# Cross attention in a two-layer decoder: the first eight heads' values and denominators from one product, with slots, sends and bias moved on GpSimd

## Chip, cores, metric

The kernel runs on one NeuronCore of a Trainium2 chip. The metric is the device time of one execution in microseconds (us). Engines are called TensorE (PE, with its weight loads PEld), VectorE (DVE), ScalarE (ACT), GpSimd (POOL) and SyncE (SP). Each has its own instruction stream, runs it in order, and waits for semaphores that others count up.

## The reference

The input x is 8 batches of 256 tokens of width 256, in float32; a context of 77 rows per batch goes with it. The decoder has two layers, each with a self attention, a cross attention to the context and a mixture of experts (8 experts, the best 2 for each token), each with a layer norm in front and a residual. The change lies in the cross attentions, 16 heads of 16 columns:

```python
q = (query @ wq.T + bq)...; k = (key @ wk.T + bk)...; v = (value @ wv.T + bv)...
scores = einsum('bhqd,bhkd->bhqk', q, k) / sqrt(HD)
attn = softmax(scores)
ctx = einsum('bhqk,bhkd->bhqd', attn, v)
return ctx @ wo.T + bo
```

## The kernel before

`attention_crossed` runs once per layer (names L0x and L1x, 237 to 362 us and 1094 to 1232 us of the trace with what surrounds it). A unit u is half a batch: b = u // 2 is the batch and c = u % 2 the half of the heads, eight in each. Five engine programs go through u = 0 to 15 side by side.

TensorE's order in a unit is: scores of unit u+1 (L827), transposes of the maxima (L837), the products of the list `mid`, then the turned scores of u, laid out with the 77 keys on the partitions (L850), and the values. The values of a first half (c = 0) come behind the turned scores of the second half; the values of a second half come ahead of the turned scores of the next batch's first half. Everything goes through a ring of seven PSUM banks, and the values have one bank more, `ps_o`. A values group (L865) is eight products with `v_s`, whose weights hold two heads for 32 rows of output, and eight with `half_ones`, which sum the exponentials into the denominators, the same rows 256 columns further on. Each product gives two records.

The other products are: `q`, `v` and `x` for the batches ahead (L300, L288, L293), `k` for a group of batches (L282), the projection `o` of batch b-1 in the second half (L797), and three steps of the router: `r0` transposes the normalized rows (L804), `r1` gives the logits (L809), `r2` counts how many tokens went to each expert (L815).

VectorE in unit u takes the maximum of scores u+1 (L468), adds the shift of u into `q_m` (L475), copies keys, takes statistics, and then: in a first half `slots(b-3)`, and behind it the orders and snapshots of the experts (`ORDER_BY = 2`, so at b = 5; `FULL_BY = [3, 4]`, at b = 6 and 7); in a second half `choose(b-2)` (best two experts), `add(b-1)` (residual L498, statistics L501, L506). Last in each unit are the sums of unit u-1: a reciprocal of the denominators (L480) and the product into `o_t` (L483). `slots` makes from gates (L536 to L538) and counts (L541 to L546) each token's row in the expert table. After the last unit come `slots(5)`, the first expert rows, `last_sums` (L490, L491), the hidden rows of the first early expert block, `choose(6)` and `add(7)`.

ScalarE takes products out of PSUM, normalizes (L205, L627) and exponentiates four banks per unit (L667). GpSimd does the small steps of the norms (L255 to L258), the bias on the residual (L725), and sends the routed rows to the table by four indirect DMAs per batch (L744). In a first half it has `spread_norm(b+2)` and `send(b-3)`; in a second half `bias(b)` and `route_norm(b-1)`.

SP's program in the stage is this loop. It stores each batch (L446), loads the first two experts' weights (L1912 to L1916) when the order is known, and for b = 4 and b = 5 waits until the batches up to 3 and 4 are scattered, then loads early expert rows (L2167):

```python
for b in range(B):
    eng.wait_ge(added, b + 1)
    eng.dma_start(... X[:, tiles, :]).then_inc(route["kept"], 16)
    if b == ORDER_BY + 1:
        experts["first_loads"](eng)
    for i, last in enumerate(FULL_BY):
        if b == last + 1:
            for par in range(2):
                eng.wait_ge(scattered[par], ((last - par) // 2 + 1) * 64)
            experts["load_early"](eng, i)
```

Behind the last unit TensorE starts on the early expert blocks while batches 6 and 7 are still being routed.

## Time and profile before

| what | us |
|---|---|
| three runs | 1500.22, 1502.38, 1503.75 (median 1502.38) |
| the profiled execution, its own time | 1504.03 |
| its span, first to last instruction | 1502.4 |
| mean granted TensorE clock | 0.993 |
| busy: PE / VectorE / ScalarE / GpSimd | 1433.9 / 748.7 / 619.1 / 490.5 |
| first cross stage, 228 to 362 | PE 122.0, VectorE 110.2, ScalarE 79.9, GpSimd 51.2 of 134 |
| second cross stage, 1078 to 1216 | PE 125.9, VectorE 109.3, ScalarE 78.1, GpSimd 51.3 of 138 |

Times in the trace count from the start of the span. A timeline row gives start, duration, engine, line, operation, output and inputs with their shapes, how many instructions it merges, and in brackets how long the engine had been idle before it and what released it. Records of TensorE overlap, because its products are pipelined. "remote" is a releaser that the profile can't name.

### The profile page before, as it was taken

What the parts mean: (1) busy time and instruction counts of PE and PEld (TensorE: products, weight loads), DVE (VectorE), ACT (ScalarE), POOL (GpSimd) and SP (SyncE); (2) the same over time, 40 slices, a digit from 0 to 9 for tenths busy, and PEclk for the clock granted to TensorE, in tenths of its full rate; (3) what the DMA queues carried; (4) which work ended last, traced back from release to release, by engine and by line L of the source; (5) the groups of instructions that cost most, each with busy time, mean ns of one, the idle gap of its engine ahead of it and who ended that gap; (6) DMA issues with size and microseconds to landing.
All of it is one profiled execution on the core that took longest, in us unless ns stands there. A gap on an engine that the chain in (4) does not pass through costs nothing. (4 is left out here: it accounts for less than half of the span.)

```text
span 1502.4 us, 34667 instructions
## 1 busy us (share of the span) xinstructions
PE 1433.9 (95%) x11880; PEld 1159.7 (77%) x11881; DVE 748.7 (50%) x2160; ACT 619.1 (41%) x1711; POOL 490.5 (33%) x758
## 2 busy tenths in 40 slices
PE   7999998988999999999999999999899899999998
PEld 5676766767899999976777777777666579999997
DVE  6666757887433333344444444444278862222222
ACT  2433346653222222235445444545366533333332
POOL 3545442444322122223233233333224452222222
PEclk9999999999999999999999999999999999999999
DMA  9920000152243434120000000000001522533332
GB/s 316 333 69 2 2 2 9 45 176 62 50 119 67 144 71 114 32 64 1 0 1 1 1 1 1 1 1 0 1 16 44 174 78 40 149 93 94 94 90 34
DMA packets 79666, 97.46 MB, mean 65 GB/s; under 512 B 10523, under 2 KB 72579, under 8 KB 79555
## 3 DMA queue, kind: packets, MB, share of 16 engines
q1 hardware_dynamic: 64643, 77.58, 16.4%
q0 software_dynamic: 13680, 17.19, 6.6%
q8 instruction: 73, 1.20, 0.3%
q10 hardware_dynamic: 1232, 1.18, 0.2%
q14 instruction: 38, 0.31, 0.1%
HBM read 57.51 MB, written 39.59 MB: 65 GB/s over the span
## 5 line engine op out<-in xcount | busy, mean ns | idle before, releaser
L1741 POOL TENSOR_TENSOR L1a_prob<-L1a_prob,L1a_rtot 128x1024 f32<-128x1024 f32 x64 | 121.1, 1892 | 275.8 <-DVE L1a_rtot L1614 275.8
L2270 PEld LDWEIGHTS L0x_ps<-L0f_rows_t,L0f_w_up 128*128 128x128 f32 x1584 | 183.7, 193 | 10.4 <-issue 9.0
L2270 PE MATMUL L0x_ps<-L0f_rows_t,L0f_w_up 128*128 128x128 f32 x1584 | 185.8, 277 | 5.6 <-issue 4.8
L2346 ACT ACTIVATE L1f_hid<-L1x_ps,L1f_b_up 128x128 f32<-128x128 f32 x296 | 92.4, 363 | 163.0 <-PE L1x_ps L2270 159.7
L2270 PEld LDWEIGHTS L1x_ps<-L1f_rows_t,L1f_w_up 128*128 128x128 f32 x1184 | 139.5, 194 | 3.4 <-issue 1.6
L2270 PE MATMUL L1x_ps<-L1f_rows_t,L1f_w_up 128*128 128x128 f32 x1184 | 140.4, 277 | 0.6 <-ACT L1f_rows_t L2330 0.6
L2279 PE MATMUL L1x_ps<-L1f_w_down,L1f_hid 128*128 128x256 f32 x592 | 134.1, 380 | 1.9 <-issue 1.9
L2214 POOL TENSOR_TENSOR turn<-eps 128x1 f32<-128x1 f32 x74 | 13.6, 184 | 372.3 <-DVE wv L2448 367.7
L1683 ACT ACTIVATE L1a_prob<-L1a_ps_s,L1a_nmax 128x256 f32<-128x256 f32 x256 | 118.2, 473 | 38.1 <-DVE L1a_nmax L1609 38.1
L2279 PEld LDWEIGHTS L1x_ps<-L1f_w_down,L1f_hid 128*128 128x128 f32 x592 | 109.6, 190 | 15.5 <-issue 2.1
L1245 POOL TENSOR_SCALAR_AFFINE_SELECT L0a_prob<-L0a_prob 128x128 f32<-128x128 f32 (+1 forms) x256 | 79.8, 353 | 104.3 <-ACT L0a_prob L1199 104.3
L2338 ACT ACTIVATE ctx_in<-L0x_ps 128x256 f32<-128x256 f32 x72 | 27.6, 383 | 183.1 <-PE L0x_ps L2270 157.1
L2279 PE MATMUL L0x_ps<-L0f_w_down,L0f_hid 128*128 128x256 f32 x432 | 99.4, 380 | 1.7 <-DVE L0f_hid L2435 1.7
L1199 ACT ACTIVATE L0a_prob<-L0a_ps 128x384 f32<-128x384 f32 x128 | 52.4, 497 | 108.0 <-PE L0a_ps L1331 108.0
L1609 DVE TENSOR_REDUCE L1a_nmax<-L1a_ps_s 128x2 f32<-128x512 f32 x128 | 79.2, 681 | 31.4 <-PE L1a_ps_s L1805 31.4
L2279 PEld LDWEIGHTS L0x_ps<-L0f_w_down,L0f_hid 128*128 128x128 f32 x432 | 79.3, 190 | 11.2 <-DVE L0f_hid L2435 1.9
L1819 PEld LDWEIGHTS L1a_ps_t<-ident,L1a_prob 128*128 128x128 f32 x500 | 59.6, 141 | 34.6 <-issue 26.3
L2435 DVE TENSOR_TENSOR L0f_hid<-ctx_in,L0x_ps 128x256 f32<-128x256 f32 x72 | 30.2, 420 | 106.0 <-ACT ctx_in L2338 70.1
L1819 PE MATMUL L1a_ps_t<-ident,L1a_prob 128*128 128x128 f32 x500 | 76.9, 276 | 3.3 <-DVE L1a_prob_t L1618 2.4
L1618 DVE COPY L1a_prob_t<-L1a_ps_t 128x512 f32<-128x512 f32 x63 | 42.8, 680 | 58.3 <-PE L1a_ps_t L1819 58.3
L1693 ACT ACTIVATE L1a_prob_t<-L1a_ps_t 128x512 f32<-128x512 f32 x62 | 37.1, 598 | 81.5 <-PE L1a_ps_t L1819 81.5
L2425 DVE TENSOR_SCALAR token<-L1f_from_end 128x1 int32<-128x1 f32 x37 | 5.7, 153 | 126.8 <-DMA out_dram<-wv,token 126.8
(486 smaller groups left out, 2812.5 us busy)
## 6 DMA issues: line engine op xcount, KB each, us to landing
expert_table<-zero SPq DMA_DIRECT2D x1, 16640.0 KB, 68.5
L0f_w_up<-in_w_dram SPq DMA_DIRECT2D x8, 1408.0 KB, 6.8
L1f_w_up<-in_w_dram SPq DMA_DIRECT2D x8, 1024.0 KB
L1f_w_down<-in_w_dram SPq DMA_DIRECT2D x8, 1024.0 KB
L0f_w_down<-in_w_dram SPq DMA_DIRECT2D x8, 768.0 KB, 8.7
L1f_rows<-expert_table SPq DMA_DIRECT2D x35, 130.0 KB
L0f_rows<-expert_table SPq DMA_DIRECT2D x32, 130.0 KB
sums<-X SPq DMA_DIRECT2D x8, 256.0 KB
```

The costliest lines, as they stand in the source:

```text
L1199: eng.activation(prob[u % 2][:, r, :, :], bank("p", u, r)[:, 0:KT * W].rearrange("p (t w) -> p t w", t=KT), ACT.Exp).then_inc(exp_done, 1)
L1245: ins = eng.affine_select(out=p, in_=p, compare_op=ALU.is_ge, fill=0.0, base=base, pattern=[[0, 2], [sign, n]], channel_multiplier=-sign)
L1609: eng.tensor_reduce(nmax[:, j % RING, :], src, AX.X, ALU.max, negate=True).then_inc(max_done, 1)
L1618: eng.tensor_copy(prob_t[s % 2][:, k, :], turn_bank(b, s, k)).then_inc(even_out, 1)
L1683: ins = eng.activation(prob[:, j % RING, q, :], ps_s[:, k, q * S:(q + 1) * S], ACT.Exp, bias=nmax[:, j % RING, q:q + 1], accum_out=total[: ...
L1693: eng.activation(prob_t[s % 2][:, k, :], turn_bank(b, s, k), ACT.Copy).then_inc(odd_out, 1)
L1741: eng.tensor_tensor(v, v, r.unsqueeze(2).to_broadcast([P, 2 * QT_N, S]), ALU.mult).then_inc(norm_done, 1)
L1819: ins = eng.transpose(out[:, o:o + P], prob[:, j % RING, q, c * P:(c + 1) * P], ident[:, :])
L2270: ins = eng.matmul(ps_h[c][:, o:o + P], w_up[par][:, t, w0:w0 + P], rows_t[:, t, :], start=(t == 0), stop=(t == DT - 1))
L2279: ins = eng.matmul(ps_y[:, 0:D], hid[:, c, k * P:(k + 1) * P], w_down[par][:, 2 * c + k, :], start=(c == 0 and k == 0), stop=(c == CHUNKS ...
L2346: ins = eng.activation(hid[:, c, k * P:(k + 1) * P], ps_h[c][:, k * P:(k + 1) * P], ACT.Gelu, bias=b_up[par][:, 2 * c + k:2 * c + k + 1])
L2435: ins = eng.tensor_tensor(hid[:, c, :], mid[:, c, :], ps_h[c][:, 2 * P:4 * P], ALU.mult)
```

## The change

For the first eight heads `v_s` now holds values and ones in turn, and one group of eight products gives values and denominators together: half of the rows of each product are values, half are sums, and the other half-product has them the other way round. ScalarE copies both (`gather`) into SBUF, SP moves the sums and the values with two DMAs each to the rows where they belong (`move`), VectorE takes the reciprocal (`sums_first`), and GpSimd multiplies (`first_outputs`). The rows of `wo` and the bias of v are reordered on the host to match (`in_turn`). The second eight heads keep the old form with interleaved rows. VectorE keeps the gates, GpSimd gets the rest of `slots` for batches 0 to 4, first in its unit; `send` is split in two, tile 0 in the first half and tile 1 in the second behind `route_norm`, and the bias comes last. VectorE's sums of a second half stand ahead of the expert order and the snapshots. SP no longer loads the first weights; ScalarE issues them in units 11 and 12.

```diff
-            eng.wait_ge(v_cleared, b % 2 + 1)
+            eng.wait_ge(v_cleared, 2 * (b % 2 + 1))
             if values_free is not None:
                 eng.wait_ge(*values_free)
-            ins = eng.activation(even_odd(v_s[b % 2][0:SC, :, :]), bank[0:SC, 0:D].rearrange("p (a two d) -> p a two d", two=2, d=DH), ACT.Copy)
...
-        eng.memset(v_s[i][:, :, :], 0.0).then_inc(v_cleared, 1)
+
+        eng.memset(v_s[i][:, 0:HEADS // 2, :], 1.0).then_inc(v_cleared, 1)
+        eng.memset(v_s[i][:, HEADS // 2:HEADS, :], 0.0).then_inc(v_cleared, 1)
...
+                def move(b):
+
+                    eng.wait_ge(copied, b + 1)
+                    if b:
+                        eng.wait_ge(rsum_done, b)
+                    for w in range(HALVES):
+                        eng.dma_start(summed_t[1 - w::2, :], gathered[w::2, w, :]).then_inc(sums_moved, 16)
+                    if b:
+                        eng.wait_ge(first_out, b)
+                    for w in range(HALVES):
+                        eng.dma_start(valued_t[1 - w::2, :], gathered[1 - w::2, w, :]).then_inc(values_moved, 16)
+
+                move(0)
                 for b in range(B):
+                    if b + 1 < B:
+                        move(b + 1)
                     eng.wait_ge(added, b + 1)
                     tiles = slice(b * QT_N, (b + 1) * QT_N)
                     eng.dma_start(route["sums"].rearrange("(t p) d -> p t d", p=P)[:, tiles, :], X[:, tiles, :]).then_inc(route["kept"], 16)
-                    if b == ORDER_BY + 1:
-                        experts["first_loads"](eng)
                     for i, last in enumerate(FULL_BY):
                         if b == last + 1:
                             for par in range(2):
...
+                def sums_first(b):
+                    eng.wait_ge(sums_moved, 32 * (b + 1))
+                    if b:
+                        eng.wait_ge(first_out, b)
+                    eng.reciprocal(rsum_first[:, :], summed_t[:, :]).then_inc(rsum_done, 1)
+
                 def sums(u):
                     b, c = part(u)
                     eng.wait_ge(values_done, u + 1)
                     linked(eng.reciprocal(rsum[:, :], ps_o[:, S:2 * S]))
-                    if c == 0 and b:
+                    if b:
                         eng.wait_ge(projected, b)
...
+                        eng.wait_ge(slot_done, b)
...
+                def gates(b):
...
+                    gate = xr[:, b % 2, :, GATE:GATE + TOP]
                     linked(eng.tensor_scalar(first_gate[:, :], odds[:, :], 1.0, None, ALU.add))
                     linked(eng.reciprocal(gate[:, :, 0], first_gate[:, :]))
-                    eng.tensor_tensor(gate[:, :, 1], gate[:, :, 0], odds[:, :], ALU.mult)
+                    eng.tensor_tensor(gate[:, :, 1], gate[:, :, 0], odds[:, :], ALU.mult).then_inc(gates_done, 1)
...
+                    gates(b)
+                    eng.wait_ge(slot_done, b)
...
+                        if b:
+                            sums_first(b - 1)
                         if b + 2 < B:
                             first["statistics"](eng, b + 2)
                         if b >= 3:
-                            slots(b - 3)
+                            gates(b - 3)
+                        if b:
+                            sums(u - 1)
+                        if b >= 3:
...
-                        if u == units - 1:
-                            sums(u - 1)
                         if b >= 1:
                             add(b - 1)
-                    if u and u < units - 1:
-                        sums(u - 1)
                 slots(B - 3)
+                sums_first(B - 1)
                 x["take_early"](0)
                 last_sums()
...
+                def gather(b):
+
+                    eng.wait_ge(values_done, CHUNKS * b + 1)
+                    if b:
+                        eng.wait_ge(sums_moved, 32 * b)
+                        eng.wait_ge(values_moved, 32 * b)
+                    eng.activation(gathered, ps_o[:, :].rearrange("p (w s) -> p w s", w=HALVES), ACT.Copy).then_inc(copied, 1)
+
...
+                    if c == 1:
+                        gather(b)
                     if u == units - 1:
                         x["table"]()
                     for t in of(END, u):
                         take(t)
+                    for e in range(2):
+                        if u == 2 * (ORDER_BY + 3) + 1 + e:
+                            experts["first_load"](eng, e)
                     if c == 0 and b + 2 < B:
...
+                def first_outputs(b):
+
+                    eng.wait_ge(values_moved, 32 * (b + 1))
+                    eng.wait_ge(rsum_done, b + 1)
+                    if b:
+                        eng.wait_ge(projected, b)
+                    eng.tensor_tensor(o_t[:, 0, :], valued_t, rsum_first, ALU.mult).then_inc(first_out, 1)
...
+                    taken = route["taken"]
+                    eng.wait_ge(both_done, b + 1)
+                    wait_out(eng, "r2", b)
+                    for q in range(QT_N):
+                        eng.tensor_tensor(place[:, q, :], counts[:, 0, q, :], taken[:, :], ALU.add)
+                        linked(eng.tensor_tensor(taken[:, :], counts[:, 1, q, :], taken[:, :], ALU.add))
+                    linked(eng.tensor_tensor(picked[:, :, :, :], chosen[:, :, :, :],
+                                             place[:, :, :].unsqueeze(1).to_broadcast([P, TOP, QT_N, EXPERTS]), ALU.mult))
+                    for n in (4, 2):
+                        linked(eng.tensor_tensor(picked[:, :, :, 0:n], picked[:, :, :, 0:n], picked[:, :, :, n:2 * n], ALU.add))
+                    linked(eng.tensor_tensor(slot_f[:, :, :], picked[:, :, :, 0], picked[:, :, :, 1], ALU.add))
+                    eng.tensor_copy(slot_i[:, b % 2, :, :], slot_f[:, :, :].rearrange("p k t -> p t k")).then_inc(slot_done, 1)
...
+                    eng.wait_ge(gates_done, b + 1)
...
+                        if b >= 3:
+                            slots(b - 3)
+                        if b:
+                            first_outputs(b - 1)
                         if b + 2 < B:
                             first["spread_norm"](eng, b + 2)
                         if b >= 3:
-                            send(b - 3)
+                            send(b - 3, [0])
                     else:
-                        bias(b)
                         if b >= 1:
                             route_norm(b - 1)
+                        if b >= 3:
+                            send(b - 3, [1])
+                        bias(b)
                 x = experts["pool_parts"](eng)
+                first_outputs(B - 1)
...
-                        eng.wait_ge(o_out, CHUNKS * (t[1] + 1) - last)
+                        eng.wait_ge(first_out, t[1] + 1)
+                        if not last:
+                            eng.wait_ge(o_out, t[1] + 1)
...
+                    flat = v_s[b % 2][0:SC, :, :].rearrange("p h n -> p (h n)")
+                    if c == 1:
+                        eng.wait_ge(copied, b + 1)
+                    elif b:
+                        eng.wait_ge(o_out, b)
+                    for summed in range(c + 1):
                         for w in range(HALVES):
                             for r in range(GROUPS):
-                                lhs = half_ones[0:SC, w, :] if summed else v_s[b % 2][0:SC, c * 8 + 2 * r + 1 - w, :]
-                                ins = eng.matmul(ps_o[rows(r), summed * S:(summed + 1) * S], lhs, prob[u % 2][0:SC, r, w * S:(w + 1) * S],
-                                                 start=(w == 0 and not summed), stop=(w == HALVES - 1), skip_group_check=True)
+                                o = (summed if c else w) * S
+                                n = 2 * DH * (c * 8 + 2 * r + 1 - w) - (1 - w)
+                                lhs = half_ones[0:SC, w, :] if summed else flat[:, n:n + 2 * DH]
+                                ins = eng.matmul(ps_o[rows(r), o:o + S], lhs, prob[u % 2][0:SC, r, w * S:(w + 1) * S],
+                                                 start=(c == 0 or w == 0 and not summed), stop=(c == 0 or w == HALVES - 1), skip_group_check=True)
                     ins.then_inc(values_done, 1)
 
...
-    def first_loads(eng):
+    def first_load(eng, e):
 
         eng.wait_ge(listed["ordered"], 1)
-        for e in range(2):
-            load_weights(eng, e, e)
+        load_weights(eng, e, e)
 
...
-                eng.memset(half_ones[:, w, 16 * (1 - w):16 * (2 - w)], 1.0).then_inc(halves, 1)
+                eng.memset(half_ones[:, w, 1 - w::2], 1.0).then_inc(halves, 1)
...
-        env.update(y=wv0[:, 0, :])
+        env.update(y=wv0[:, 0, :], rsum_first=wv0[:, 1, :], gathered=wk0[:, :, :], summed=wo0[:, 0, :], valued=wo0[:, 1, :])
...
+    def in_turn(w):
+
+        return w.reshape(-1, 2, 16, *w.shape[1:]).swapaxes(1, 2).reshape(w.shape)
```

## Rows read from the trace of the kernel before

**Rows 1.** The page, part 1: busy us, share of the span, instructions.
```profile
PE 1433.9 (95%) x11880; PEld 1159.7 (77%) x11881; DVE 748.7 (50%) x2160; ACT 619.1 (41%) x1711; POOL 490.5 (33%) x758
```
**Rows 2.** Busy time by stretch: PE, PEld, DVE, ACT, POOL, clock, DMA share, GB/s.
```profile
252.00:267.00 15.00, 14.75 (x180) 10.46 (x176) 12.01 (x31) 10.02 (x21) 3.85 (x9) 1.00 0.06 20
...
1208.00:1214.00 6.00, 4.95 (x38) 2.95 (x39) 5.07 (x21) 1.68 (x5) 2.44 (x5) 0.57 0.25 83
```
**Rows 3.** Timeline, batches 6 and 7 of the first layer.
```profile
334.32 1.10 PE L850 MATMUL L0x_ps<-L0x_q_m,L0x_k_m 32*77 32x256 f32 x16 [1.78 <-DVE L0x_q_m L475]
...
339.49 1.43 DVE L468 TENSOR_REDUCE L0x_tops<-L0x_ps 128x16 f32<-128x1232 f32 x1
...
340.84 0.68 DVE L475 TENSOR_TENSOR L0x_q_m<-L0x_q_m,L0x_ps 128x512 f32<-128x512 f32 x1
...
348.07 1.10 PE L850 MATMUL L0x_ps<-L0x_q_m,L0x_k_m 32*77 32x256 f32 x16
...
353.46 1.07 PE L865 MATMUL L0x_ps_o<-L0x_prob,L0x_v_s 77*32 77x256 f32 x16 [1.61 <-DVE L0x_o_t L483]
```
**Rows 4.** Timeline, batches 4 and 5: the expert order and what waited.
```profile
309.45 0.16 DVE L1963 TENSOR_TENSOR L0r_tokens<-taken,regions 128x8 f32<-128x8 f32 x1
...
312.53 0.15 DVE L1976 TENSOR_SCALAR L0r_least<-L0r_least 128x1 f32<-128x1 f32 x1
...
315.08 1.97 PE L797 MATMUL L0x_ps<-wo,L0x_o_t 128*128 128x256 f32 x8 [2.12 <-DVE L0x_o_t L483]
...
317.41 1.10 PE L850 MATMUL L0x_ps<-L0x_q_m,L0x_k_m 32*77 32x256 f32 x16
...
318.53 2.04 ACT L667 ACTIVATE L0x_prob<-L0x_ps 77x512 f32<-77x512 f32 x4 [0.41 <-PE L0x_ps L850]
```
**Rows 5.** The bank of the values by instruction: ns min/median/max, first and last start.
```profile
L865 PE MATMUL L0x_ps_o<-L0x_prob,half_ones x256: 378/379/380, 238.7 to 355.0; 77*32 77x256 f32 x128
...
L480 DVE RECIPROCAL L0x_rsum<-L0x_ps_o x15: 1722/1756/1758, 239.8 to 351.1; 128x256 f32<-128x256 f32 x15
L483 DVE TENSOR_TENSOR L0x_o_t<-L0x_ps_o,L0x_rsum x15: 423/424/425, 241.6 to 352.9; 128x256 f32<-128x256 f32 x15
```
**Rows 6.** GpSimd's lines, ns min/median/max; an early load, KB and us to landing.
```profile
L725 POOL TENSOR_TENSOR X<-X,bo x16: 1265/1272/1290, 234.2 to 1203.8; 128x512 f32<-128x512 f32 x16
...
L255 POOL TENSOR_TENSOR L0x_r_veps<-L0x_r_mv,eps x8: 194/194/195, 253.1 to 367.1; 128x2 f32<-128x2 f32 x8
...
L744 POOL DMA_INDIRECT expert_table<-L0x_xr,L0x_slot_i x32: 959/966/1244, 277.1 to 382.9; - x32
...
ctx_in<-expert_table SPq DMA_DIRECT2D x8, 130.0 KB, 2.1
```
**Rows 7.** Timeline, the router's norm of batch 5.
```profile
337.16 0.25 DVE L506 BATCH_NORM_AGGREGATE L0x_r_mv<-L0x_r_stats 128x2 f32<-128x6 f32 x2
...
338.84 0.22 POOL L258 TENSOR_SCALAR L0x_r_shift_by<-L0x_r_offset 128x2 f32<-128x2 f32 x1
```
**Rows 8.** Timeline, the last send of batch 3 and SP's next issue.
```profile
330.42 0.96 POOL L744 DMA_INDIRECT expert_table<-L0x_xr,L0x_slot_i  x1 [0.30 <-issue]
...
333.70 0.89 SPq L2167 DMA_DIRECT2D ctx_in<-expert_table  x2
```
**Rows 9.** The copy of the experts' numbers, ns min/median/max.
```profile
L522 DVE CAST L0x_index_f<-L0x_index x8: 169/170/1782, 265.8 to 374.6; 128x4 f32<-128x4 uint32 x8
```
**Rows 10.** SP's issues of the first experts' weights, both layers.
```profile
313.34 0.38 SPq L1913 DMA_DIRECT2D L0f_w_down<-in_w_dram  x1
...
315.48 0.02 SPq L1912 DMA_DIRECT2D L0f_w_up<-in_w_dram  x1
...
1174.97 4.22 SPq L1915 DMA_DIRECT2D L1f_b_up<-in_b_dram  x1
```
**Rows 11.** Timeline behind the last unit: last sums, batch 7's router rows.
```profile
356.49 0.95 DVE L490 RECIPROCAL L0x_rsum<-L0x_ps_o 128x128 f32<-128x128 f32 x1
...
369.99 0.63 PE L804 MATMUL L0x_ps<-ident,L0x_xr 128*128 128x128 f32 x4 [0.20 <-ACT L0x_xr L627]
```

More of the change, by code:

```diff
@@ L138, in batches_of @@
         return b0, b1, b1 - b0
-    def even_odd(v):
-        return v.rearrange("p (a two) (half d) -> p a (two half) d", two=2, half=2)[:, :, 0::3, :]
     def weights_in(eng):
@@ L374, in attention_crossed @@
         apart, odds, first_gate = sb("apart", [P, QT_N]), sb("odds", [P, QT_N]), sb("first_gate", [P, QT_N])
+        gathered, summed_t, valued_t, rsum_first = (env[k] for k in ("gathered", "summed", "valued", "rsum_first"))
         cleared = sem("cleared")
+        gates_done, link_p = sem("gates_done"), sem("link_p")
+        copied, sums_moved, values_moved = sem("copied"), sem("sums_moved"), sem("values_moved")
+        rsum_done, first_out = sem("rsum_done"), sem("first_out")
         scores_done, max_done = sem("scores"), sem("max")
@@ L529, in choose @@
                     eng.tensor_copy(xr[:, par, :, TOKEN], route["from_end"][:, b * QT_N:(b + 1) * QT_N])
+                def gates(b):
+                    eng.wait_ge(odds_done, b + 1)
+                    gate = xr[:, b % 2, :, GATE:GATE + TOP]
+                    linked(eng.tensor_scalar(first_gate[:, :], odds[:, :], 1.0, None, ALU.add))
+                    linked(eng.reciprocal(gate[:, :, 0], first_gate[:, :]))
+                    eng.tensor_tensor(gate[:, :, 1], gate[:, :, 0], odds[:, :], ALU.mult).then_inc(gates_done, 1)
                 def slots(b):
                     par, taken = b % 2, route["taken"]
-                    eng.wait_ge(odds_done, b + 1)
-                    gate = xr[:, par, :, GATE:GATE + TOP]
-                    linked(eng.tensor_scalar(first_gate[:, :], odds[:, :], 1.0, None, ALU.add))
-                    linked(eng.reciprocal(gate[:, :, 0], first_gate[:, :]))
-                    eng.tensor_tensor(gate[:, :, 1], gate[:, :, 0], odds[:, :], ALU.mult)
+                    gates(b)
+                    eng.wait_ge(slot_done, b)
                     wait_out(eng, "r2", b)
@@ L566, in _ @@
                         if b >= 3:
-                            slots(b - 3)
+                            gates(b - 3)
+                        if b:
+                            sums(u - 1)
+                        if b >= 3:
+                            if b == 3 and not final or b - 3 == ORDER_BY or b - 3 in FULL_BY:
+                                eng.wait_ge(slot_done, b - 2)
                             if b == 3 and not final:
@@ L633, in odds_of @@
                     if b:
-                        eng.wait_ge(slot_done, b)
+                        eng.wait_ge(gates_done, b)
                     eng.wait_ge(apart_done, b + 1)
@@ L858, in values @@
                     wait_out(eng, "v", b)
-                    if u:
-                        eng.wait_ge(o_out, u)
-                    for summed in range(2):
+                    flat = v_s[b % 2][0:SC, :, :].rearrange("p h n -> p (h n)")
[4 more added lines that the diff above has]
+                    for summed in range(c + 1):
                         for w in range(HALVES):
                             for r in range(GROUPS):
-                                lhs = half_ones[0:SC, w, :] if summed else v_s[b % 2][0:SC, c * 8 + 2 * r + 1 - w, :]
-                                ins = eng.matmul(ps_o[rows(r), summed * S:(summed + 1) * S], lhs, prob[u % 2][0:SC, r, w * S:(w + 1) * S],
-                                                 start=(w == 0 and not summed), stop=(w == HALVES - 1), skip_group_check=True)
+                                o = (summed if c else w) * S
[3 more added lines that the diff above has]
+                                                 start=(c == 0 or w == 0 and not summed), stop=(c == 0 or w == HALVES - 1), skip_group_check=True)
                     ins.then_inc(values_done, 1)
```

17 lines of the change are left out of this document (12 added, 5 removed).

## The prediction, made before the changed kernel ran

> **What bounds the kernel now.** The page comes first: TensorE (PE) is busy for 1434 of 1502 us [rows 1], so the program is nearly PE-bound. Then the view of busy time by stretch: in the first cross attention, 252 to 267 us, PE is busy 14.75 of 15 us, while GpSimd has 3.85 and VectorE 12.0 [rows 2]. There a PE instruction removed is time won. The other end of the stage is different. The timeline shows PE waiting: 2.12 us for the scaled outputs of VectorE before L797, 1.78 us for the shift before L850, and 1.61 us for `o_t` before the last values [rows 3, 4]. So from batch 5 on what counts is who comes late, and I read both crosses (237 to 362 us and 1094 to 1232 us) batch by batch. I call R the start of the turned scores of a batch's second unit (317.41, 334.32 and 348.07 for batches 5, 6, 7) [rows 3, 4].
>
> **Products removed.** For the first eight heads the second group of products with `half_ones` goes: 16 records of 379 ns each, overlapping four at a time [rows 5]. The group at 353.46 spans 1.07 us [rows 3], with the tail of its last product, which the next one runs under; four at a time make 16 x 379 / 8 = 0.76 us at least. I take 0.93 us per batch (bounds 0.76 and 1.07), nearer to the span. The group stands just after R.
> Batches 0 to 2: PE is the bound, VectorE, ScalarE and GpSimd have room. The new path must be in time: ScalarE's copy 128x512 comes behind the exponentials, which end at R+3.2 (318.53+2.04) [rows 4]; the copy has no row of its own here, bounds are 0.42 (the 256-column read of the same bank on VectorE [rows 5]) and 1.27 (512 columns on GpSimd [rows 6]); I take 0.6, since the exponential of 512 columns takes 0.51 (2.04/4). SP issues two DMAs, they land after 2.1 us (130 KB [rows 6]; 64 KB may do it in less, 3 us under load is the upper bound), at R+6.3. The reciprocal on VectorE from SBUF: 1.75 us from PSUM [rows 5], I take the same; bounds 0.9 and 1.8. It ends at R+8.1; the statistics and sums of the other half end at R+11.5; L797 wants them at about R+11.7. Just in time: **3 x 0.93 = -2.8 us** per layer (0 if landing takes 3 us).
>
> **Work moved to GpSimd.** Slots: nine dependent instructions; an instruction of two columns takes 0.195 us there, 512 columns 1.27 [rows 6], so 0.2 to 0.26 each, with gaps 2.3 us. The outputs' product of 256 columns: between, (1.27+0.195)/2 = 0.73. Per batch GpSimd then has 2.3+0.73, two norms of 1.6 (337.41 to 339.06 [rows 7]), sends 4x1.27 = 5.1 (0.97 and a gap of 0.30 [rows 6, 8]), bias 1.27: 12.5 us in a period of 14.8. That fits, with about 2 us spare; the bias last frees the router's norm. The bias collision on VectorE (a cast of 1782 ns instead of 169 [rows 9]) goes away, but stood beside PE's work: 0.
> Batch 3: the router's rows hang on the keys' products, which are not moved; PE waited for them already, so the 0.93 only lengthens that wait: 0.
> Batch 4 into 5: the expert order on VectorE, 309.45 to 312.68 = 3.2 us [rows 4], stood before the sums and made PE wait 2.12. Now it stands behind them, but ahead of the next maximum (1.43) and shift (0.68) [rows 3]: they end at R+17.2 against 18.0 before: **-0.8**, in the second layer **-0.9**.
>
> **Expert weights issued by ScalarE.** In unit 11 the load stands ahead of the router's norm. On SP 1.8 us passed from the end of the first expert's issues (313.72) to the second's first (315.48), most of it the load of the expert's number, and two issues take about 0.8; in the second layer there are four issues, and one of them stood for 4.22 us with the queue full [rows 10]. So ScalarE gets to the norm 2 to 4 us late, and PE's L804 with it. Against that stands batch 5's 0.93 and the 1.78 us wait before L850. I take **-0.8** in the first layer and **+1.1** in the second.
>
> **What is queued behind SP's waits.** This decides. SP's program runs: move(b+1), wait for added(b), store, and for b=4 and 5 a wait for the scatters of batches up to 3 and 4, then the early expert rows. Before, nothing urgent stood behind that wait. Now move(6) and move(7) do. And what it waits for became later: tile 1 of batch 3 is sent only in unit 13, behind the router's norm. Numbers for batch 6 (R=334.32): the aggregate ends at R+3.1 (337.16+0.25) [rows 7], norm 1.6, two sends to R+7.1. From the end of the last send to SP's next issue it was 2.3 us (331.38 to 333.70), and the two loads took 0.9 [rows 8]: SP is free at R+10.4, issues, and the sums land at R+12.8. VectorE gets there at about R+5.2: the shift ended at 341.52 = R+7.2, behind a sum of 2.17 us that is gone [rows 3, 5] (0.2 allowed for what comes in between). It waits **7.5 us** in the one queue that also holds gates, the other sums, snapshot and the last shift. From 12.8: reciprocal 1.75, gates 0.6, sum 2.2, so `o_t` at R+17.4; L797 can't start before; snapshot 0.9 and shift 0.7 end at 19.1. Before, the batch took 348.07-334.32 = 13.75 [rows 3]; now 19.2: **+5.5 us** per layer. Nothing covers it: L797 and the turned scores behind it are all that PE has left in the unit.
> Batch 7 repeats it: send(4) tile 1 leaves at R+7.0, SP is free at 10.2, sums land at R+12.7. They stand ahead of `last_sums`, which began at 356.49 = R+8.4 [rows 11] and now begin at R+14.5; the expert products' hidden rows stand behind them. PE has up-products, r0 and r1 until about R+12; the last router rows were turned at 369.99 = R+21.9 [rows 11]; behind GpSimd's send(5) (from R+15.2 to 20.3), odds and norm they come at R+24.7: **+2.8 us**. The 1.61 us that the last values waited [rows 3] are won, but only in front of that wait.
> Clock: after such a hole PE fell to the lower level (1.2 GHz): mean 0.57 in 1208 to 1214 [rows 2], where the last values stood. That costs 0 to 3.4 us a layer more than before; I take **+1.0**.
>
> **Sum.** First layer -2.8-0.8-0.8+5.5+2.8+1.0 = +4.9; second -2.8-0.9+1.1+5.5+2.8+1.0 = +6.7; together +11.6. The profiled execution took 1504.0 (span 1502.4), so 1515.6; the three runs' median is 1502.4, 1.6 lower: **1514**.
>
> A rule against the change: the Trainium skill, DMA: Bandwidth & Descriptors (Anatomy of one DMA), says that a semaphore wait happens on the issuing sequencer before dispatch, not in the DMA engines. By this rule everything behind SP's wait stands still; were it not so, the +5.5 and +2.8 would be 0.
>
> **Rivals.**
> (A) *The blocked queue costs little* and the savings show. For it: PE is the bound in most of the stage. Against: VectorE is in order, and the sums are asked for before all else in the unit. It would take the sends landing by R+6. Then batches 0 to 2, 4 and 5 keep their gain and the last values come 1.6 us sooner: -6.0 and -4.2, so **1492**. Chance 0.17.
> (B) *VectorE's reciprocal now holds GpSimd up*, on top of the forecast. Its source and its result are in SBUF now. A cast of VectorE stood 1.6 us too long beside GpSimd's bias [rows 9], so the engines can block each other. If GpSimd's bias waits 1.15 us in batches 3 to 6, its 2 us of room go, and the xn and slot path adds about 0.9 a batch: 4x0.9x2 = +7, **1521**. Chance 0.13.
> The Trainium skill, SBUF — State Buffer (SBUF: two separate sides), has such a rule: a pair of ports that VectorE and GpSimd share is locked for a whole instruction. The trace agrees for the cast, 1782 against 169 ns; for a long reciprocal no row shows it.
> (C) *It evens out*: the block is half as long, because the last scatter lands sooner than the 2.3 us [rows 8] and GpSimd sends it earlier. Half of 2x8.3 is 8.3 less, and with it the clock's 2.0: 1514-10.3 = 1503.7, **1504**. Chance 0.10.
>
> **Chances.** Forecast 0.60. A measurement of this kernel can tell about 0.2%, 3.0 us, from no change. Slower: forecast and B, 0.73; same: C, 0.10; faster: A, 0.17. The range goes from 1499 (landing 2.1 us, shorter block, no clock loss) to 1525 (B and two clock drops); it leaves out A.
>
> **What would show it.** Right: VectorE idle 6 to 8 us before the new reciprocal in the units after batches 6 and 7, released by a DMA from `wk0`'s columns, in both layers; SP's issues of these moves directly behind the early expert rows; PE's hole in front of L797 of batch 6; batch periods shorter by 0.9 us for batches 0 to 2. Wrong: those moves issued within 1 us of their copies (then A), or GpSimd idle nowhere and VectorE waiting for its product (then B), or unit 11's norm on time.

## The result, and the profile after

Three runs of the changed kernel took 1581.32, 1582.49 and 1587.34 us, against 1500.22, 1502.38 and 1503.75 before: a ratio of 1.054 (95% interval 1.051 to 1.058), 80 us slower. The forecast was 1514 with a range to 1525. The sign was right, but 68 us of the 80 were not in it; as e1 and e9 below show, the sign too owed most to effects that the forecast had small or at nothing. The profiled execution is the one of 1582.49 us, with a span of 1580.8.

The page of the changed kernel, part 1 (busy us, share of the span, instructions):

```profile
span 1580.8 us, 34355 instructions
PE 1468.0 (93%) x11624; PEld 1178.9 (75%) x11625; DVE 734.2 (46%) x2074; ACT 625.8 (40%) x1727; POOL 520.6 (33%) x868
```

TensorE has 256 records fewer than in [rows 1], 128 products at two records each, and is busy 34 us longer. Next, busy time by stretch, from the start of the first cross stage to the first down-product of the experts (columns as in [rows 2]). The kernel before:

```profile
228.00:365.20 137.20, 125.18 (x1412) 89.40 (x1411) 111.79 (x320) 80.60 (x171) 52.71 (x87) 0.99 0.22 76
```

The changed kernel, with 10 us from the middle of it:

```profile
228.00:401.80 173.80, 137.54 (x1282) 94.57 (x1281) 103.74 (x278) 83.80 (x179) 67.49 (x140) 0.83 0.22 72
340.00:350.00 10.00, 5.78 (x48) 2.98 (x52) 3.17 (x5) 3.81 (x7) 3.17 (x6) 0.50 0.45 159
```

The same work takes 36.6 us more. 24.2 of them are idle time of TensorE (36.3 against 12.0), and 12.4 are products that run longer although there are fewer: the mean granted clock is 0.83. The last row, the 10 us around the end of an idle stretch of 9.2 us (it ends at 344.22), has a granted clock of 0.50 throughout, the lower level (1.2 GHz). The second layer loses 42 us.

I compare batch by batch, by the time from the turned scores R of a batch's second unit to those of the next. The rows are starts of L850 (L938 after), subtracted:

```
                  batch 0->1   1->2   2->3   3->4   4->5   5->6   6->7
before, layer 1      14.80  14.95  16.01  16.81  18.03  16.91  13.75
after,  layer 1      15.48  14.08  15.15  27.20  21.32  26.65  22.29
before, layer 2      14.80  14.94  16.02  16.97  16.76  16.92  13.74
after,  layer 2      14.76  14.21  15.15  27.91  24.12  29.85  21.98
```

Up to batch 3 the kernel is a little faster, by 1.0 and 1.6 us per layer where the forecast had 2.8. From the first batch in which sends run beside routing, each period is 3 to 13 us longer. What TensorE waits for there is named by the view of waits, first layer, changed kernel (us in total, times, longest):

```profile
PE L0x_ps L892 <- ACT L0x_xr L662: 24.1, 5, 9.2
PE L0x_ps_o L897 <- DVE L0x_o_t L517: 5.1, 1, 5.1
```

L892 turns the normalized router rows (`r0`), L662 is ScalarE's normalization. The view of L662 says what ScalarE waited for:

```profile
L662 ACT ACTIVATE L0x_xr<-X,L0x_r_shift_by,L0x_r_rstd x16: 584/599/617, 255.1 to 405.5; 128x256 f32<-128x256 f32 x16
...
  DMA expert_table<-L0x_xr,L0x_slot_i: 28.2, 5
  DMA expert_table<-L1x_xr,L1x_slot_i: 25.6, 5
```

and the timeline of batch 5, first layer, shows how:

```profile
332.06 0.25 DVE L532 BATCH_NORM_AGGREGATE L0x_r_mv<-L0x_r_stats 128x2 f32<-128x6 f32 x2
332.92 0.42 ACTq L2005 DMA_DIRECT2D L0f_w_up<-in_w_dram  x1
332.95 1.10 SPq L456 DMA_DIRECT2D wo<-wk  x2
333.75 0.23 POOL L256 TENSOR_SCALAR L0x_r_shift_by<-L0x_r_offset 128x2 f32<-128x2 f32 x1
334.78 1.06 POOL L823 DMA_INDIRECT expert_table<-L0x_xr,L0x_slot_i  x1 [0.81 <-issue]
336.15 0.96 POOL L823 DMA_INDIRECT expert_table<-L0x_xr,L0x_slot_i  x1 [0.30 <-issue]
337.13 1.27 POOL L773 TENSOR_TENSOR X<-X,bo 128x512 f32<-128x512 f32 x1
340.34 1.75 DVE L501 RECIPROCAL wv<-wo 128x256 f32<-128x256 f32 x1 [5.47 <-DMA wo<-wk]
342.98 1.09 ACT L662 ACTIVATE L0x_xr<-X,L0x_r_shift_by,L0x_r_rstd 128x256 f32<-128x256 f32 x2 [9.88 <-DMA expert_table<-L0x_xr,L0x_slot_i]
344.22 1.08 PE L892 MATMUL L0x_ps<-ident,L0x_xr 128*128 128x128 f32 x4 [9.20 <-ACT L0x_xr L662]
345.23 1.94 PE L958 MATMUL L0x_ps_o<-L0x_prob,L0x_v_s 77*32 77x256 f32 x16
```

The router's rows live in two buffers, `xr[b % 2]`. ScalarE may write the rows of batch b only when those of batch b-2 have been scattered (`wait_ge(scattered[par], b // 2 * 64)` in its `route_norm`). Before, all four sends of batch b-3 left in the first half of a unit pair, and by the time of the norm of batch b-1 they had long landed. Now GpSimd issues tile 1 behind its own `route_norm(b-1)`, so ScalarE, whose next instruction is the normalization of that very batch, waits for the issue (from the shift at 333.98 to 337.11) and the landing (to 342.9). The landing is slow in this batch, 5.8 us, with the first expert's weights under way (the DMA engines are 0.92 busy from 335 to 344.2); in batch 6, without them, it took 1.7 us and ScalarE still waited 4.53. All that TensorE has behind L892 waits with it, and then runs at half clock: a values group takes 1.94 us instead of 1.07.

### The profile page after: what moved, and what is told of

It reads as the page before. It is cut to its first block and busy times, and to the rows that moved or that the text cites. A ratio compares the mean times of both kernels' runs of the same rounds, so it can differ in the third digit from the quotient of the medians.

```text
span 1580.8 us, 34355 instructions
## 1 busy us (share of the span) xinstructions
PE 1468.0 (93%) x11624; PEld 1178.9 (75%) x11625; DVE 734.2 (46%) x2074; ACT 625.8 (40%) x1727; POOL 520.6 (33%) x868
## 5 line engine op out<-in xcount | busy, mean ns | idle before, releaser
L2371 PEld LDWEIGHTS L0x_ps<-L0f_w_down,L0f_hid 128*128 128x128 f32 x432 | 79.6, 191 | 10.9 <-DVE L0f_hid L2527 1.7
L1201 DVE TENSOR_REDUCE L0a_tops<-L0a_ps 128x2 f32<-128x384 f32 x128 | 62.5, 552 | 11.6 <-PE L0a_ps L1407 11.6
```

What stands on the lines that cost most here:

```text
L1201: eng.tensor_reduce(tops[u % UNITS][:, :, at_row], src, AX.X, ALU.max, negate=True).then_inc(max_done, 1)
L2371: ins = eng.matmul(ps_y[:, 0:D], hid[:, c, k * P:(k + 1) * P], w_down[par][:, 2 * c + k, :], start=(c == 0 and k == 0), stop=(c == CHUNKS ...
```

## The experiments

I call W the theory that this wait makes the loss, and S the one of the forecast, SP's blocked queue. All edits are to the changed kernel unless it is said. The kernel before ran again beside each group of experiments: its medians are 1499.5 (e1 to e4), 1501.3 (e6 to e8), 1503.6 (e9, e10) and 1499.6 (e11, e12). A difference between kernels of different groups carries this drift of up to 4 us, so I also give the distance to the kernel before of the same group. That distance was 80.1 us for the changed kernel. "Batch 5's period" is the column 5->6 of the table above. e2, e3 and e4 are single executions.

**e1: sends together.**

```diff
-                            send(b - 3, [0])
+                            send(b - 3)
...
-                        if b >= 3:
-                            send(b - 3, [1])
```

> Edit: the changed kernel with all four sends of batch b-3 in the first half again; nothing else. Theory W: what costs the 78 us is ScalarE's normalization of a batch's router rows, which waits until the rows of two batches before have been scattered out of the same buffer; these scatters now leave in the same unit behind the router's norm on GpSimd. Then that wait goes: 1490 to 1505 us, and PE waits under 2 us per layer for the normalized rows instead of 24.1 and 22.3. Theory S: the moves behind SP's wait for the scatters hold VectorE up and that carries the loss. Here the scatter of batch 3 lands before the move of batch 6 too, so S also expects about 1500. This run alone does not tell W from S. A third theory (C): the loss is the moved slots and products on GpSimd or the contention of its port with VectorE; then it stays above 1560.

Measured: 1507.84 (ratio 1.0056, 1.0038 to 1.0073), 8.4 us above the kernel before. 72 us of the 80 are gone with this one edit. It lies inside the forecast's range, but not for the forecast's reasons, as the next runs show.

**e2: three buffers in the first layer.** `xr`, `slot_i` and `scattered` have three entries, used by `b % 3`, in the first layer; the second keeps two.

```diff
-        xr, xr_t = sb("xr", [P, 2, QT_N, ROW]), sb("xr_t", [P, DT, S])
+        xr, xr_t = sb("xr", [P, 2 if final else 3, QT_N, ROW]), sb("xr_t", [P, DT, S])
```

> Edit: the changed kernel with three buffers for the router's rows and slots in the first layer only; the sends stay apart, so SP's waits and the place of each send are as changed. The second layer keeps two buffers, as a control. W: ScalarE's wait for a scatter goes in the first layer and stays in the second: 28 to 36 us off the 1582, so 1546 to 1554; the second layer's batches keep their 22 to 30 us periods. What then stays in the first layer is S's part: VectorE's wait of 5 to 8 us for the moved sums of batches 6 and 7. S (SP's blocked queue carries most): at most 5 us off, 1577 or more.

Measured: 1560.34. It is 22 us less, not 28 to 36; the first layer's seven periods are 21.4 us shorter. The view of ScalarE's normalization has no wait for a scatter left in the first layer, and the control is untouched:

```profile
  DMA expert_table<-L1x_xr,L1x_slot_i: 24.5, 5
  POOL L0x_r_shift_by L256: 5.2, 4
```

What stays in the first layer is largely S, now in the open. VectorE's reciprocal of the moved sums, batches 5, 6 and 7:

```profile
328.70 1.75 DVE L501 RECIPROCAL wv<-wo 128x256 f32<-128x256 f32 x1 [5.54 <-DMA wo<-wk]
350.32 1.75 DVE L501 RECIPROCAL wv<-wo 128x256 f32<-128x256 f32 x1 [7.88 <-DMA wo<-wk]
371.94 1.75 DVE L501 RECIPROCAL wv<-wo 128x256 f32<-128x256 f32 x1 [4.35 <-DMA wo<-wk]
```

In batches 6 and 7 SP issued the moves 7.26 and 6.20 us behind ScalarE's copy, which is S. In batch 5 it issued them 0.03 us behind it, so the 5.54 us are not S (e6 shows what they are). The forecast had 7.5 us for batch 6. The period from batch 6 to 7 is 21.96 us against 13.75 before, 8.2 more where the forecast took 5.5, and the first down-product starts at 380.6 instead of 365.2, 15 us late.

**e3: the kernel before with its sends parted.**

```diff
-                            send(b - 3)
+                            send(b - 3, [0])
                     else:
                         bias(b)
                         if b >= 1:
                             route_norm(b - 1)
+                        if b >= 3:
+                            send(b - 3, [1])
```

> Edit: the kernel before, with only the sends parted: tile 1 of batch b-3 in the second half, behind the router's norm. There are no moves on SP here. W: the whole loss without the rest of the change: 60 to 80 us above the kernel before, 1560 to 1582, with PE waiting 20 to 25 us per layer for the normalized rows. S: nothing urgent stands behind SP's wait, so within 4 us of 1502.

Measured: 1571.21, 72 us above the kernel before, with nothing else of the change in it. The periods from batch 3 on are 26.83, 17.57, 26.60 and 21.53. The normalization, line by its two layers:

```profile
  DMA expert_table<-L0x_xr,L0x_slot_i: 29.0, 5
  DMA expert_table<-L1x_xr,L1x_slot_i: 28.9, 5
```

72 from this edit and 8 from all the rest (e1) make the 80. W is shown by taking the wait away in two ways (e1 by the place of the sends, e2 by a third buffer) and by adding it alone.

**e4: early rows one batch later.** SP's wait for the scatters and the loads behind it stand behind the next `move`.

```diff
-                        if b == last + 1:
+                        if b == last + 2:
```

> Edit: the changed kernel, with SP's wait for the scatters and the early loads one batch later, behind the next move; sends stay apart. W: ScalarE's wait is untouched, so little is won: 1572 to 1582; PE still waits 20 us or more per layer for the normalized rows, and only VectorE's 5 to 8 us waits for the moved sums go. S: 1500 to 1515.

Measured: 1569.16, 13 us less (10 by the distances): more than W allowed, far from S. The normalization still waits 26.0 us in the first layer. VectorE's waits for the sums of batches 6 and 7 are gone (0.68 and none instead of 8.36 and 5.47), but that of batch 5 is 7.00, so it had another cause. The first layer's periods are no shorter for it (142.1 us in sum, 142.2 in the changed kernel), since ScalarE's wait covers them; what is won lies mostly behind the last turned scores, where the first down-product comes 15.2 us after the R of batch 7 instead of 23.5, and 15.2 instead of 20.3 in the second layer.

**e6: the first weights behind the move.** e1, and SP issues both experts' weights behind the store of batch 4.

```diff
+                    if b == ORDER_BY + 2:
+                        for e in range(2):
+                            experts["first_load"](eng, e)
...
-                        if u == 2 * (ORDER_BY + 3) + 1 + e:
-                            experts["first_load"](eng, e)
```

The rows that led to it, e1's timeline: ScalarE's weights and SP's moves of batch 5 leave in the same microsecond, and the sums land 6.6 us after their second issue.

```profile
319.03 0.42 ACTq L2003 DMA_DIRECT2D L0f_w_up<-in_w_dram  x1
319.06 1.10 SPq L456 DMA_DIRECT2D wo<-wk  x2
...
326.21 1.75 DVE L501 RECIPROCAL wv<-wo 128x256 f32<-128x256 f32 x1 [5.23 <-DMA wo<-wk]
```

> Edit: sends together as in e1, and the first two experts' weights no longer issued by ScalarE in units 11 and 12 but by SP behind the store of batch 4, so behind the move of batch 5 in its queue. Theory M: in e1 the moves of batch 5 (64 KB each) were issued at the same moment as the first expert's weights (2.2 MB) and landed 6.6 us later instead of 1.9, which made VectorE wait 5.2 and 5.9 us, and in the second layer ScalarE's issues of four loads took 5.1 us and held the normalization up by 5.2. Then both go: batch 5's period falls from 19.07 and 24.99 to 16.5 to 17.5 us, together 8 to 11 us off e1's 1507.8: 1496 to 1500. Rival N: the waits come from VectorE's or GpSimd's own load (slots, blocked port); then e6 stays at 1505 to 1509.

Measured: 1506.08 (1.0023, 1.0011 to 1.0035). Batch 5 gains more than M said, 14.60 and 14.61 us instead of 19.07 and 24.99. But batch 6 now takes 19.79 and 21.01, so only 1.8 us are won (3.6 by the distances) and the number is missed. The burst has moved on to the next victim, as the second layer shows: in 10 us with the DMA engines busy throughout (a DMA share of 1.03) a scatter needs 7.4 us to land, and SP is held in one issue for 6 us.

```profile
1185.00:1195.00 10.00, 6.02 (x66) 4.00 (x64) 6.91 (x22) 3.87 (x10) 6.24 (x17) 0.96 1.03 347
```

```profile
1184.67 6.01 SPq L2006 DMA_DIRECT2D L1f_b_up<-in_b_dram  x1
...
1194.23 1.09 ACT L665 ACTIVATE L1x_xr<-X,L1x_r_shift_by,L1x_r_rstd 128x256 f32<-128x256 f32 x2 [3.36 <-DMA expert_table<-L1x_xr,L1x_slot_i]
...
1199.60 1.75 DVE L504 RECIPROCAL wv<-wo 128x256 f32<-128x256 f32 x1 [7.07 <-DMA wo<-wk]
```

**e7: e6 and e4 together.**

> Edit: e6, and SP's wait for the scatters with the early rows' loads one batch later, behind the next move. If SP's block still costs something where the sends are together (e1: VectorE waited 2.9 us for the sums of batch 6, PE 3.1 us in front of the output product), this takes 2 to 5 us more off e6: 1492 to 1497. If the early rows then come too late for the early blocks, the stage's end gives it back: equal to e6 or up to 3 us above it.

Measured: 1504.68 (1.0020, 1.0007 to 1.0033), not told apart from e6. That does not show that SP's wait costs nothing. In e6 it held the moves of batch 6 for 3.6 and 5.2 us behind ScalarE's copy. In e7 they leave at once in the first layer, but beside the weights the sums need 6.0 us to land, and VectorE waits 4.67 instead of 5.71:

```profile
333.87 0.60 ACT L707 ACTIVATE wk<-L0x_ps_o 128x512 f32<-128x512 f32 x1
334.50 1.11 SPq L456 DMA_DIRECT2D wo<-wk  x2
340.99 1.75 DVE L504 RECIPROCAL wv<-wo 128x256 f32<-128x256 f32 x1 [4.67 <-DMA wo<-wk]
```

**e9: the weights apart.** e6, with one expert behind the store of batch 4 and the other behind that of batch 5.

```diff
-                    if b == ORDER_BY + 2:
-                        for e in range(2):
+                    for e in range(2):
+                        if b == ORDER_BY + 2 + e:
```

> Edit: as e6, but SP issues the first expert's weights behind the store of batch 4 and the second's behind the store of batch 5, each behind a move. In e6 both came in one burst, the DMA engines were full for 10 us, a scatter took 7.4 us to land instead of 2.6 and batch 6 needed 19.8 and 21.0 us. Theory M (the weights' transfers are what delays moves and scatters): half the burst at a time fits between the moves, batches 5 and 6 together take 32 to 33 us instead of 34.4 and 35.6, so 3 to 6 us off e6: 1499 to 1503. Rival: the early rows' load and the wait before it in the same queue hold batch 6 up as before: 1504 to 1508, and the second expert's weights, one batch later, may hold the experts' first products up.

Measured: 1502.65 (0.9994, 0.9974 to 1.0014), even with the kernel before. Batches 5 and 6 together take 32.87 and 32.29 us. M holds: the place of 4 MB of weights is worth 5 us against e1 (9 by the distances). What is left in batch 6 is in part S: SP issues the moves 2.4 us behind the copy (2.9 in the second layer), right behind the early rows, and VectorE waits 4.19 (3.53).

```profile
332.73 0.60 ACT L707 ACTIVATE wk<-L0x_ps_o 128x512 f32<-128x512 f32 x1
335.72 1.11 SPq L456 DMA_DIRECT2D wo<-wk  x2
339.37 1.75 DVE L504 RECIPROCAL wv<-wo 128x256 f32<-128x256 f32 x1 [4.19 <-DMA wo<-wk]
```

**e8: slots on VectorE again.** e6, with `slots(b - 3)` in VectorE's first halves instead of `gates`, and gone from GpSimd.

> Edit: e6 with the slots of batches 0 to 4 on VectorE again, behind the gates. Theory: VectorE is not the bound in batches 0 to 3 and 2.3 us of slots there cost nothing; in batches 5 to 7 its queue carries the order and snapshots, so 1 to 2 us each: e6 plus 0 to 4 us. Rival B (the shared port: VectorE's reciprocal from SBUF blocks GpSimd and its slots): then e8 is faster than e6 by 2 us or more.

Measured: 1511.84 (1.0070, 1.0045 to 1.0095), 5.8 us slower than e6, more than the 0 to 4 expected. The period from batch 3 to 4 is 0.9 us longer in both layers (17.68 against 16.78, 17.65 against 16.76), the next 1.1 and 0.7, and that from 5 to 6 in the first layer 2.7. The slots belong on GpSimd, and rival B is against the numbers.

**e10: the kernel before with the part that needs no transfer.** Slots on GpSimd first in the unit, the bias last, the sums of a second half ahead of the order; two groups of products, sends and SP's program as before.

```diff
                     if c == 0:
+                        if b >= 3:
+                            slots(b - 3)
...
-                        bias(b)
                         if b >= 1:
                             route_norm(b - 1)
+                        bias(b)
```

> Edit: the kernel before with only the GpSimd and VectorE part of the change that has no transfer in it: slots of batches 0 to 4 on GpSimd ahead of all else, the bias last, VectorE's sums of a second half ahead of the order and snapshots. Values and denominators stay two groups of products, sends stay together, SP's program is that of before. Theory: TensorE is the bound in batches 0 to 3, so 0 there; in batches 4 to 7 VectorE is on the path and 2.3 us of slots leave it, while the order no longer stands before the output product (2.1 us wait in the first layer): 1 to 4 us per layer, 1493 to 1499, faster than the kernel before. Rival: VectorE's and GpSimd's short instructions hold each other up, or the sends leave 2 to 3 us later behind the slots and ScalarE's normalization waits for them: 1500 to 1506.

Measured: 1497.23 (0.9961, 0.9942 to 0.9980). This beats both kernels. Its periods from that of batch 4 on are 16.58, 15.05 and 11.89 in the first layer and 15.49, 15.74 and 11.88 in the second; before batch 4 they are those of before.

**e11: ScalarE issues the moves** (e9, with `move(b)` behind `gather(b)` in ScalarE's program).

> Edit: e9, and ScalarE issues the moves itself, right behind its copy of the bank; in SP's program only stores, weights and early rows are left. Theory S (what is left of the merged product's cost in e9, 18.3 and 17.7 us from batch 6 to 7 against 13.8 before, is the move of batch 6 standing behind SP's wait for scatters and the early rows' load): the sums of batch 6 land 2 us behind the copy in both layers, that period falls to 13 to 15 us, and the time by 3 to 8 us: 1495 to 1500. Rival: ScalarE's four issues, 2.3 us by their durations in SP's queue, stand ahead of the router's norm and take it back: 1501 to 1505.

Measured: 1556.74 (1.0365), far outside both. Each period is 15 to 24 us from batch 0 on. Around the issues ScalarE does nothing else for 3.4 us in batch 0 and for 2.5 to 2.8 in batches 1 to 6, in front of the copies and exponentials that TensorE needs next. In the first layer that makes 18.9 us, of the 25.4 by which the seven periods are longer than in e9:

```profile
241.41 1.18 ACTq L692 DMA_DIRECT2D wo<-wk  x2
242.62 2.13 ACTq L696 DMA_DIRECT2D wo<-wk  x2
...
244.79 0.84 ACT L228 ACTIVATE L0x_q_raw<-L0x_ps,bq1s 128x256 f32<-128x256 f32 x2 [3.42 <-issue]
```

So SP was the better engine of the two for the moves, and the run says nothing on S: the new stall covers it.

**e12: the kernel before with the sums ahead of the order, alone.**

```diff
                         if b >= 3:
                             slots(b - 3)
+                        if b:
+                            sums(u - 1)
+                        if b >= 3:
...
-                    if u and u < units - 1:
+                    if c and u < units - 1:
                         sums(u - 1)
```

> Edit: the kernel before with one thing moved on VectorE: the sums of a second half stand ahead of the expert order and the snapshots. The forecast's term for it was 0.8 and 0.9 us (batch 4 into 5), and e10, which has it, was 0.4% faster. If the order is what e10's gain comes from: 1497 to 1499. If it is the slots on GpSimd: 1499 to 1502, with the periods of batches 6 and 7 as before (16.9 and 13.8 us).

Measured: 1499.09 (0.9992, 0.9973 to 1.0010): no difference that can be told. The profiled execution, 1503.83 us, was among the slowest of ten. Batch 4's period, in which the order stands, is 0.11 and 0.14 us shorter than before, where e10's is 1.45 and 1.27 shorter. In its second layer batches 5 and 6 are 1.9 and 0.8 us shorter; in its first batch 6 is 0.8 shorter, but batch 5 is 2.9 longer. How e10's gain divides between the slots, the bias and the order stays open; the order alone is not it.

## Why the prediction was wrong

Step by step, in the prediction's order.

*Products removed, -2.8 per layer.* The group did go, and ScalarE's copy took 0.61 us (0.6 taken) and GpSimd's product 0.73 (0.73). Batches 1 and 2 gave 0.87 and 0.86 in the first layer, 0.73 and 0.87 in the second, where 0.93 stood. Batch 0 gave nothing: 0.04 in the second layer, and 0.7 lost in the first, where the sums landed at R+8.2 (reciprocal at 244.34, R at 236.08) and not at R+6.3. So it was about 1.0 to 1.6 per layer.

*Work moved to GpSimd.* Here is the failed step. "[...] sends 4x1.27 = 5.1 [...] That fits, with about 2 us spare; the bias last frees the router's norm." The sends were costed as time on GpSimd, and their new place only for SP's wait. I did not ask who else counts `scattered`. ScalarE does, in front of the normalization. It is the wait of a writer for the reader of two batches ago. The sum has no term for it. In the trace of before it is all but free, and it shows in one place only, at the end of this line of ScalarE's groups (kernel before; busy, mean ns of one, idle before and its releasers):

```profile
L627 ACT ACTIVATE L1x_xr<-X,L1x_r_shift_by,L1x_r_rstd 128x256 f32<-128x256 f32 x16 | 8.7, 592 | 12.0 <-POOL L1x_r_shift_by L258 10.9 <-DMA expert_table<-L1x_xr,L1x_slot_i 1.1
```

That 1.1 us was the hint, and the code says the rest. Batch 3, forecast at 0, lost 10.4 and 10.9 us; in the first layer ScalarE waited 28.2 us for scatters and TensorE 24.1 us for the rows; e3 puts the whole at 72 us.

*Batch 4 into 5, -0.8 and -0.9.* Not visible in the changed kernel. In e1 the period is 1.29 and 0.77 shorter: right in size, but not by the mechanism. e12, which moves only the sums ahead of the order, makes it 0.11 and 0.14 shorter; e10, with the slots and the bias moved too, 1.45 and 1.27. The order's place alone is worth next to nothing there, and the agreement in e1 is luck.

*Expert weights issued by ScalarE, -0.8 and +1.1.* In e1 batch 5 lost 2.2 and 8.1 us. The norm's delay had been costed (2 to 4 us; ScalarE's four issues took 5.1 in the second layer). What the weights' 2.2 MB do to the transfers beside them had not: the moved sums land in 6.6 us and not in 2.1. e6 and e9 show it. The place of the weights, by the burst and by ScalarE's issues, is what made e1 slower than the kernel before: in e9, which differs from e1 in nothing else, nothing of the 8.4 us is left.

*SP's queue, +5.5 and +2.8.* The mechanism is real and was foreseen in place and form: VectorE waited 7.88 us in e2, 8.36 in the changed kernel, where 7.5 stood, and the moves left directly behind the early rows' load. For batch 7 it waited 5.47, and in the second layer 6.89 and 3.47. e2 has batch 6's period 8.2 us longer than before, where the term was 5.5. The rule cited from the Trainium skill (DMA: Bandwidth & Descriptors, Anatomy of one DMA), that a semaphore wait happens on the issuing sequencer, agrees with the timeline of the changed kernel. ScalarE's copy is done at 359.60, but SP issues nothing before the last scatter has landed, at 364.23. In e4, where that wait stands behind the move, the move leaves 0.03 us after the copy.

```profile
359.00 0.60 ACT L704 ACTIVATE wk<-L0x_ps_o 128x512 f32<-128x512 f32 x1
361.60 0.96 POOL L823 DMA_INDIRECT expert_table<-L0x_xr,L0x_slot_i  x1 [0.30 <-issue]
365.29 0.93 SPq L2259 DMA_DIRECT2D ctx_in<-expert_table  x2
366.32 1.11 SPq L456 DMA_DIRECT2D wo<-wk  x2
369.82 1.75 DVE L501 RECIPROCAL wv<-wo 128x256 f32<-128x256 f32 x1 [8.36 <-DMA wo<-wk]
```

Its size hung on the parted sends. The hold, from the copy of batch 6 to SP's issue, was 6.7 and 6.2 us in the two layers of the changed kernel; with the sends together it was 0.9 and 0.03 in e1, 3.6 and 5.2 in e6, 2.4 and 2.9 in e9. Of the 80 us S is the smaller part: e4, which takes it away, gives 10 to 13.

*Clock, +1.0 per layer.* TensorE was busy 12.4 us longer in the first layer, with fewer products and a mean granted clock of 0.83 instead of 0.99; there is now a hole in nearly every batch from 3 on.

*The rivals.* A (the block costs little) and C (it evens out) fell: VectorE waited 8.36 and 6.89 us for the moved sums of batch 6. B fell too: in the changed kernel L501 runs from 271.76 to 273.51, and GpSimd's instructions start inside it 0.28 and 0.26 us apart, as they do without it (292.38 and 292.65). The Trainium skill, SBUF — State Buffer (SBUF: two separate sides), has the shared pair locked by a VectorE instruction that runs in a 2-port mode, or that has two inputs in SBUF while GpSimd's reads SBUF. This reciprocal has one input, and the trace shows no lock by it.

```profile
271.76 1.75 DVE L501 RECIPROCAL wv<-wo 128x256 f32<-128x256 f32 x1 [0.57 <-DMA wo<-wk]
271.92 0.20 POOL L807 TENSOR_TENSOR L0x_picked<-L0x_picked 128x8 f32<-128x8 f32 x1
272.20 0.20 POOL L808 TENSOR_TENSOR L0x_slot_f<-L0x_picked 128x4 f32<-128x4 f32 x1
272.46 0.19 POOL L809 CAST L0x_slot_i<-L0x_slot_f 128x4 int32<-128x4 f32 x1
```

What happens is the other direction, and small: a VectorE product of two columns that takes 0.16 us took 0.63 beside GpSimd's product of 256 columns, and ended with it (372.46 and 372.43). Both its inputs are in SBUF, and by that rule the trace agrees: GpSimd's product started first.

```profile
371.70 0.73 POOL L781 TENSOR_TENSOR L0x_o_t<-wo,wv 128x256 f32<-128x256 f32 x1 [5.67 <-issue]
371.83 0.63 DVE L563 TENSOR_TENSOR L0x_xr<-L0x_xr,L0x_odds 128x2 f32<-128x2 f32 x1
```

*What the merged product is worth.* e9 against e10 is the merged product with its moves, apart from where the first weights are issued: 5.4 us slower in the medians. It wins 1.5 and 2.4 us in the six periods up to batch 6 and loses 6.4 and 5.8 us in the period from batch 6 to 7, where the moved sums (VectorE waits 4.19 us for them) stand in front of the output product. Of the first layer's 4.19 us, 2.4 are SP's late issue; the rest is issuing and landing. What would be left of that loss if the move landed at once stays open. e7 lets it leave at once, but beside the weights; e11 put the issues on an engine that had no room; e9 with SP's wait behind the next move was not run.

## What to carry to other kernels

When an instruction that signals a semaphore is moved, list every waiter on that semaphore in the code, the writers that reuse its buffer above all; a wait that is free before hardly shows in a trace, and moving its signal by half a batch cost 72 us here. An in-order queue that gets an urgent entry should have no wait and no large transfer ahead of it: move the large transfers to where no small one is under way, and in pieces. Work moved without a transfer in its path (e10: the slots on GpSimd, the bias last, the sums ahead of the order) gave 0.4%; the product that saved 0.9 us and added a round trip by DMA did not.

## What the hardware showed that I had not expected

- A move of 64 KB within SBUF took 1.9 us to land in the median (e1, 64 moves), and up to 7.3 beside the experts' weights; a scatter took 2.6 in the median and 7.4 in e6 with the DMA engines full.
- Issuing four DMAs kept ScalarE from work for 2.5 to 3.8 us (e11, first layer); SP has no arithmetic in its program that the same issues could displace.
- With the DMA engines busy throughout (share 1.03 from 1185 to 1195 in e6), one issue stood for 6.0 us on SP, as 4.22 in [rows 10]; the issues of weights next to it took 0.4 to 0.5 us. What holds the issue is not shown.
- The reciprocal of 256 columns takes 1.75 us from SBUF (L501) as from PSUM (L506).
